# Attention block with group norm on one core: finer waits on stored outputs, and sums, snapshots and splits in another order

## The reference

```python
h = group_norm(x, gamma, beta)                    # 32 groups, eps 1e-6
q, k, v = conv1x1(h, wq, bq), conv1x1(h, wk, bk), conv1x1(h, wv, bv)
attn = softmax(einsum('bci,bcj->bij', q, k) * 512 ** -0.5)
out = conv1x1(einsum('bcj,bij->bci', v, attn), wo, bo)
return x + out
```

## Time and profile before

| | us |
|---|---|
| median of 3 runs | 2030.69 |
| lowest and highest | 2030.28, 2032.45 |
| the profiled execution, its own time | 2031.8 |
| the profiled execution, its span | 2029.9 |
| TensorE busy | 1985.6 (98%) |
| VectorE busy | 1630.4 (80%) |
| ScalarE busy | 999.5 (49%) |
| GpSimd busy | 325.8 (16%) |

### The profile page before, as it was taken

How to read it: one execution, slowest core, us unless ns; L and a number is a source line. 1 busy time by engine, 2 the same in 40 slices (tenths; PEclk the granted TensorE clock), 3 DMA queues, 4 the chain that set the end, 5 groups by cost and what they waited for, 6 DMA issues and landing times.

```text
span 2029.9 us, 29828 instructions
## 1 busy us (share of the span) xinstructions
PE 1985.6 (98%) x9924; PEld 1678.9 (83%) x9924; DVE 1630.4 (80%) x2284; ACT 999.5 (49%) x1529; POOL 325.8 (16%) x241
## 2 busy tenths in 40 slices
PE   9999999999999999999999999999999999999998
PEld 7787878878788787887878878787887878878887
DVE  7897787978879688696887969778797887978856
ACT  6464453645536464453644536445364553646443
POOL 2012120111202012020221201212011120201202
PEclk9999999999999999999999999999999999999999
DMA  6436152363424535154350533615236242363402
GB/s 238 150 146 162 60 163 93 145 165 124 102 84 151 159 145 124 42 176 134 145 155 31 174 116 145 159 74 150 93 145 165 98 119 93 146 164 145 86 28 42
DMA packets 55467, 255.45 MB, mean 126 GB/s; under 512 B 8208, under 2 KB 8208, under 8 KB 50832
## 3 DMA queue, kind: packets, MB, share of 16 engines
q1 hardware_dynamic: 34896, 221.53, 28.7%
q0 software_dynamic: 18432, 33.56, 11.1%
q10 hardware_dynamic: 2112, 0.01, 0.1%
HBM read 214.18 MB, written 74.45 MB: 142 GB/s over the span
## 4 chain that ended last, share of the span: by engine, by line
PE 81%; DVE 7%; DMA 7%; issue 3%; ACT 2%; POOL 0%; DVEq 0%; SPq 0%; POOLq 0%; ACTq 0%
PE psum L406 27%; PE psum L407 27%; PE psum L408 27%; DMA out<-scores 6%; DVE h_lo L955 3%; DVE scores L1186 1%; ACT scores L749 1%; DVE scores L1028 1%; DVE wide L1179 0%; DVE red L1174 0%; ACT scores L704 0%; DVE big_lo L1053 0%; DMA scores<-in_wq 0%; DVE bn L886 0%; DVE big_lo L1139 0%
## 5 line engine op out<-in xcount | busy, mean ns | idle before, releaser
L406 PE MATMUL psum<-big_hi 128*128 128x512 f32 x1056 | 411.9, 390 | 2.8 <-POOL big_lo L348 2.8
L407 PE MATMUL psum<-big_lo,big_hi 128*128 128x512 f32 x1056 | 411.9, 390 | 0.0
L408 PE MATMUL psum<-big_hi,big_lo 128*128 128x512 f32 x1056 | 411.5, 390 | 0.0
L406 PE MATMUL psum<-big_hi,h_hi 128*128 128x512 f32 x896 | 350.7, 391 | 3.9 <-ACT room L815 3.2
L407 PE MATMUL psum<-big_lo,h_hi 128*128 128x512 f32 x896 | 349.4, 390 | 0.0
L408 PE MATMUL psum<-big_hi,h_lo 128*128 128x512 f32 x896 | 349.3, 390 | 0.0
L1118 DVE TENSOR_TENSOR scores<-psum,room 128x512 f32<-128x512 f32 x192 | 130.7, 689 | 185.3 <-ACT room L815 135.3
L408 PE MATMUL psum<-w_split,h_lo 128*128 128x256 f32 x896 | 253.6, 283 | 0.0
L407 PE MATMUL psum<-w_split,h_hi 128*128 128x256 f32 x896 | 253.6, 283 | 0.0
L406 PE MATMUL psum<-w_split,h_hi 128*128 128x256 f32 x896 | 253.5, 283 | 0.0
L815 ACT COPY room<-psum 128x512 f32<-128x512 f32 x192 | 112.8, 587 | 275.5 <-PE psum L408 275.5
(11 more groups left out here) (133 smaller groups left out, 3448.2 us busy)
## 6 DMA issues: line engine op xcount, KB each, us to landing
w_split<-kept_t SPq DMA_DIRECT2D x15, 3584.0 KB, 11.8
w_split<-kept_v SPq DMA_DIRECT2D x15, 3584.0 KB, 11.3
room<-in_x SPq DMA_DIRECT2D x64, 512.0 KB, 3.4
out<-scores POOLq DMA_DIRECT2D x128, 256.0 KB, 6.8
room<-in_x SPq DMA_DIRECT2D x60, 256.0 KB, 4.7
red<-in_x SPq DMA_DIRECT2D x30, 256.0 KB, 4.6
wide<-in_x SPq DMA_DIRECT2D x30, 256.0 KB, 8.3
kept_t<-w_split SPq DMA_DIRECT2D x1, 3584.0 KB, 11.0
```

The source lines that it names most:

```text
L406: nc.tensor.matmul(o, a_hi, b_hi, start=start, stop=False, skip_group_check=True)
L407: nc.tensor.matmul(o, a_hi, b_lo, start=False, stop=False, skip_group_check=True)
L408: return nc.tensor.matmul(o, a_lo, b_hi, start=False, stop=stop, skip_group_check=True)
```

## The change

- `make_t` no longer waits for four stores at a time. Each sum waits for the store of the output whose slot it overwrites: r = 0's D3, D1, D2 and B11 for outputs 0 to 3, r = 1's D2, B11, B22 and B21 for outputs 4 to 7. The second D3 and D1 wait for no store.
- The first D3 of the next image (`begin_t`) is issued on VectorE ahead of the scaling of outputs 4 to 7.
- In `later_parts` ScalarE does snapshot "b" and D3's high part before the biases of outputs 4 to 6, and the bias of output 7 after snapshot "y".
- In the first image ScalarE makes the last four high parts of the weights after S's first six snapshots and first two copies. VectorE's four low parts follow its sums C22, and the statistics of the six pieces and three of the maxima come after the sums C21.
- The row products of wo and bv move into the first image's T, read wo where it still lies, and bv is loaded once wv is split; four loads of wo are gone.
- The last image's last output goes another way: x's block is loaded into a free buffer, VectorE adds output, bias and x in one instruction, and SyncE's queue stores the result without adding in memory.

```diff
+            sp.wait_ge(wv_split, KC)
+            sp.dma_start(bv_rows, bv.partition_broadcast(P)).then_inc(bv_in, 16)
...
-                    for c in range(KC):
-                        sp.dma_start(wo_again[c], w_d["o"][:, c, :]).then_inc(wo_back, 16)
-                    sp.dma_start(bv_rows, bv.partition_broadcast(P)).then_inc(bv_in, 16)
...
+                else:
+                    sp.wait_ge(h_split, count(b, 7, 7))
+                    sp.dma_start(rest, x_d[b][:, KC - 1, HALF:N]).then_inc(rest_held, 16)
+                    sp.wait_ge(rest_in, count(b, 16, 16))
+                    sp.wait_ge(last_added, 1)
+                    sp.dma_start(out_d[b, KC - 1, :, HALF:N], scaled(2 * KC - 1)).then_inc(last_stored, 16)
...
                 for r in range(2):
                     if r == 0:
                         snap(b, r, 0, "a", T_AT[4])
-                        for n in (KC, KC + 1):
+                    snap(b, r, 1, "b", T_AT[2])
+                    high_t(b, r, "D3")
+                    if r == 0:
+                        for n in range(KC, 2 * KC - 1):
                             bias_output(b, n, last=True)
-                    snap(b, r, 1, "b", T_AT[2])
+                    snap(b, r, 2, "y", T_AT[6])
                     if r == 0:
-                        for n in (KC + 2, KC + 3):
-                            bias_output(b, n, last=True)
-                    high_t(b, r, "D3")
-                    snap(b, r, 2, "y", T_AT[6])
+                        bias_output(b, 2 * KC - 1, last=True)
...
                             nc.scalar.copy(snap_s(q, n), bank[alpha_s[q % 2]][:]).then_inc(s_snapped, 1)
-                            if first and pair == 0 and n < 2:
-                                high_wv(3 + 2 * n + q)
...
+                    if first and pair == 0:
+                        for n in range(3, 7):
+                            high_wv(n)
...
+            def row_dots(c):
+                if c:
+                    dve.wait_ge(bv_used, c)
+                nc.vector.tensor_tensor_reduce(out=wo_bv_terms, in0=wo_raw[:, c, :], in1=bv_rows, scale=1.0,
...
             def make_first_t():
+                low_h(0, 1, True)
+                low_h(0, 2, True)
+                dve.wait_ge(bv_in, 16)
+                dve.wait_ge(vec_in, 16 * len(vec_d))
+                for c in (0, 1):
+                    row_dots(c)
+                low_h(0, 3, True)
+                sum_h(0, 2, True)
...
+            def left(b, n):
+                dve.wait_ge(out_stored[n], count(b, 16, 0))
+
+            def begin_t(b):
+                left(b, 0)
+                add_t(b, 0, "D3")
+
             def make_t(b):
-                for n in range(KC):
-                    dve.wait_ge(out_stored[n], count(b, 16, 0))
-                add_t(b, 0, "D3")
                 low_t(b, 0, "D3")
+                left(b, 1)
                 add_t(b, 0, "D1")
+                left(b, 2)
                 add_t(b, 0, "D2")
+                left(b, 3)
                 add_t(b, 0, "B11")
...
-                for n in range(KC, 2 * KC):
-                    dve.wait_ge(out_stored[n], count(b, 16, 0))
                 add_t(b, 1, "D3")
...
                 add_t(b, 1, "D1")
+                left(b, 4)
                 add_t(b, 1, "D2")
+                left(b, 5)
                 add_t(b, 1, "B11")
+                left(b, 6)
                 add_t(b, 1, "B22")
+                left(b, 7)
                 add_t(b, 1, "B21")
...
                 inverse(b, 1)
+                if more:
+                    begin_t(b + 1)
                 for n in range(KC, 2 * KC):
                     output(b, n)
+                if not more:
+                    dve.wait_ge(o_scaled, count(b, 8, 4 * KC))
+                    dve.wait_ge(rest_held, 16)
+                    nc.vector.scalar_tensor_tensor(scaled(2 * KC - 1), scaled(2 * KC - 1), out_bias[:, KC - 1:KC], rest,
+                                                   ALU.add, ALU.add).then_inc(last_added, 1)
```

More of the change, by code:

```diff
@@ L394, in image @@
                 pool.wait_ge(rest_in, count(b, 16, 16))
-                for n in range(2 * KC):
+                for n in range(2 * KC if more else 2 * KC - 1):
                     half, c = divmod(n, KC)
@@ L1063, in make_first_t @@
                 add_t(0, 1, "D3", True)
+                for c in (2, 3):
+                    row_dots(c)
+                dve.wait_ge(bv_used, KC)
+                nc.vector.tensor_tensor(out_bias[:], wo_bv[:], bo_s, ALU.add).then_inc(biases_set, 1)
                 low_h(0, 6, True)
@@ L1256, in image @@
                     dve.wait_ge(s_added, count(b, 12, ADD_AT["C11", q1]))
-                    for j in (q0, q1) if pair else (q1,):
-                        maximum(b, step, j)
-                        step += 1
+                    late = first and pair == 0
+                    if not late:
+                        for j in (q0, q1) if pair else (q1,):
+                            maximum(b, step, j)
+                            step += 1
                     add_s(b, "C21", q0)
@@ L1262, in image @@
                     dve.wait_ge(s_added, count(b, 12, ADD_AT["C21", q1]))
-                    for j in (KC + q0, KC + q1):
+                    if late:
+                        for n in range(6):
+                            next_piece(b, n)
+                        dve.wait_ge(bn_set, PIECES + 6)
+                    for j in ((q1,) if late else ()) + (KC + q0, KC + q1):
                         maximum(b, step, j)
                         step += 1
-                    if first and pair == 0:
-                        first_bias()
                 centre(b, 0, 0)
```

48 lines of the change are left out of this document (17 added, 31 removed).

## The result

The changed kernel takes **1978.05 us** (median of 4 runs, 1977.16 to 1979.9) against 2030.49 us (2029.89 to 2032.45): a ratio of 0.9741, 95% interval 0.9724 to 0.9758, so 52.4 us faster. The forecast was 1979.4 us, between 1976 and 1988. The profiled execution took 1977.69 us, its span is 1975.6 us, 54.3 less than before.

The account below looks back on a forecast made before the run. TensorE, busy for 1985.6 of 2029.9 us, bounds the kernel, so only its idle and slow time can be won. 43.8 + 1.9 + 4.8 + 0.8 = 51.3 us off 2030.7 gives 1979.4 us, range 1976 to 1988.

Parts of the forecast that it names:

- Step 1: T's second D3 on VectorE: without the stores TensorE's 1.34 us wait goes; B21's store stays hidden by 0.9 us.
- rival (d): In T, stores of outputs 5 to 7 slow further, B21 and then S wait: slower, up to 2040 us; 3%.
- Rival (c): In T, stores weren't what held D3; the second runs as late as before for its snapshot or product: 2001.5 us; 3%.
- Steps 2 and 3: In T, snapshot "b" is ready at 787.4, before product 6 at 787.9; the first D3 runs at 786.2, before 789.58.
- Step 4: In T, snapshot "y" behind three biases is done at 790.4, product 3 comes at 790.6: it fits by 0.2 us.
- Rival (a): VectorE or ScalarE is 1 us later in T, so "y" costs some 0.9 us in fourteen images: 1992 us; 12%.
- T in sum: The fifteen later T stages: 46.8 us of excess less 15 x 0.2 us left in, a gain of 43.8 us.
- The residue: Time still lost in T, some 0.1 us at product 2 behind snapshot "a"; 0.2 us per T left for such losses.
- Smoother S: S stages behind a late D3 fall from 38.23 to 38.08 us: 13 x 0.15 = 1.9 us gained.
- Step 5: Image 0: snapshots first remove TensorE's wait in S, V and O start without a wait; 3.7 to 5.1 us, taken as 4.8.
- the prediction's own sign: Image 0: Step 5 counts as wrong if TensorE idles between 60 and 115 us.
- Step 6: The kernel's end: the last store, issued by SyncE, lands at 2027.8 us, 0.8 us gained (between 0 and 0.9).

Follow-up runs that it names:

- the first experiment: The kernel before, with each sum of T waiting only for its own slot's store, all else in the old order: 1998.83 us against 2031.83, ratio 0.9836.
- the longer copy: The changed kernel with an extra ScalarE copy of 128 x 880 elements ahead of snapshot "y" in the first half of each T: 1986.73 us.

## Why the prediction was right, and where a term was off

- **Step 1, the second D3:** right. It waits for its product and for no DMA. The later sums' waits are covered as said: the last store lands 18.7 us into T (laid out: 801.4 against a T start of 782.45, 19.0), B21 runs 1.4 us after it (laid out: 0.9), and S has no wait. The range's danger, rival (d), didn't come about, and the experiments show why the store is slow (the loads beside it). Rival (c) was priced too low: it took 22.1 us for the D3 waits, and the first experiment shows 33 for them.
- **Steps 2 and 3:** right together. The experiments add what the forecast had not said: neither stands on its own.
- **Step 4, the tight place:** it fits, as said, but the cover was mis-sized: 0.2 us laid out, with nothing in it for the way from ScalarE to TensorE, 0.40 us measured beside a way of 0.06. The snapshot ends 7.84 us into T (laid out: 7.95), and product 3 is due at 8.30 (8.15), because product 2 already restarts behind a wait. Rival (a) fell with it. Its price was of the right size: the longer copy, 0.84 us, cost 0.58 us in each T, 8.7 us in all.
- **T in sum:** 43.8 foreseen, 44.6 measured. The residue is 0.14 us per T, not 0.2, and it lies where I put it: product 2, behind snapshot "a", takes 1.48 us in place of 1.36. Smoother S: 1.9 foreseen, 1.8 measured.
- **Step 5, image 0:** the failed sentence is "V and O start without a wait now, and I take 4.8 us". The 5.1 us in S came in full, but V gave back 0.8 us in the profile and 1.8 us in its repetition, so the term was worth 4.3 and 3.3 us. By the prediction's own sign the step failed: TensorE idles 0.57 us at 104.68. The mechanism stood in the calculation of the lower bound: a last maximum 3.7 us earlier against TensorE's 5.1 leaves VectorE 1.4 us short, and ScalarE's queue hands that on to TensorE in V. Measured, the maximum is 3.6 us earlier in the first profile and 2.7 in the repetition, so 3.7 was the best case and no bound; in seven of the nine profiles V alone takes the term below it. The row products cost nothing in T of image 0, as said (19.04 us before and after).
- **Step 6, the end:** the mechanism was right and the term mis-sized, 0.8 foreseen, 2.3 to 2.5 measured. I took an undisturbed load's 2.9 us for the store's landing, which is 2.0; and I had no term for the time after the landing, which fell from 1.18 to 0.47 us. That no store from SyncE's queue is in the trace is wrong: two of 3584 KB are, the one to `kept_t` landing in 11.0 us, but none of this size.
- **The start,** 1.1 us, was in no term and doesn't belong to the change. All profiles of this study, of either kernel, have the first S between 53.69 and 56.40. So a part of the good match in the total is luck.

Sum by the steps: 51.3 foreseen, 53.2 measured without the start in this profile; T was too low by 0.8 us and step 6 by 1.7, step 5 too high by 0.5 (by 1.5 in the repetition), and these partly cancel.

The Trainium skill's page DMA: Bandwidth & Descriptors, section Anatomy of one DMA, gives 2.0 us plus the bytes at 436 GB/s for a DMA issued by GpSimd, an estimate of 2.6 us for this size. Issued by GpSimd without accumulation and without neighbours it took 2.3 us, which bears the estimate out roughly. With accumulation it was 3.7 us, and 5.5 (no loads beside it) to 9.4 us in T, which is where this kernel's time lay. Rival (c), which followed from that figure, fell with the first experiment.

## What to carry to other kernels

A group of waits in front of one instruction is as late as its latest: give each reader the one wait that its own buffer needs, and look at the engine's queue rather than at the sum of busy time for what stands behind it. An in-order queue makes edits depend on each other: here two reorderings win 13.5 us in T together and lose 7 and 13 us if one is taken without the other, and with one group of waits left in place the kernel with all other edits is slower than the one it came from. Where an engine's new deadline was laid out by hand, insert small extra instructions of two lengths to measure the cover, and read the start of the waiting instruction: the total time mixes missing cover with the price of the restart.

## What the runs showed of the hardware that I had not expected

The same gap can end at either clock. Behind GpSimd's first parts TensorE waits 2.8 to 3.0 us at about 24 us in every profile. Two executions, the changed kernel's first profile and its repetition:

```profile
24.32 0.47 PE L416 MATMUL psum<-big_hi 128*128 128x512 f32 x1 [2.93 <-POOL big_lo L358]
```

```profile
23.52 0.73 PE L416 MATMUL psum<-big_hi 128*128 128x512 f32 x1 [2.79 <-POOL big_lo L358]
24.05 0.63 PE L417 MATMUL psum<-big_lo,big_hi 128*128 128x512 f32 x1
24.48 0.63 PE L418 MATMUL psum<-big_hi,big_lo 128*128 128x512 f32 x1
```

In the first the matmuls behind it run at 2.4 GHz; in the second they begin 0.43 us apart, the level of 1.2 GHz, for 3.5 us (granted clock 0.81 from 23 to 32 us), and in the kernel with the snapshot moved in V until 29.6 us (0.63), with the same code there. From the wait to the first T these three executions take 11.0, 12.6 and 13.8 us, so the half clock costs 1.6 and 2.8 us, a part of the spread of the kernel's runs. The kernel before had 12.6 us there in its profile (granted clock 0.81 from 23 to 32 us), the changed kernel 11.0: that is 1.6 us, and since the wait ended 0.6 us earlier in the kernel before (23.76 against 24.32), 1.1 us are left, the start's term. The other surprise is the 0.7 us at the very end: after the last landing the span goes on for 1.18 us in the five profiles where GpSimd issued the last store and for 0.47 us in the nine where SyncE did. Why is left open; no run took it apart.
